# A two-layer graph network on one core: features and first weight ahead of the basis ring, earlier turns, basis parts in pairs

## What is computed

```python
# x [625, 512]; 20625 edges (src, dst, type); D = 512, R = 2 relations, 30 bases
h  = A_norm @ (x @ W0.T) + b            # graph convolution, normalised adjacency
h  = gelu(batch_norm(h)) + x
x  = layernorm(x + h)
def rgcn(x, basis, att, gate_w, root, bias):
    w = einsum('rb,bio->rio', att, basis)       # basis: 30 x 512 x 512 fp32
    msg = sigmoid(x_j @ gate_w[r]) * x_j @ w[r] # x_j: features of each edge's other end
    return segment_sum(msg) + x @ root + bias
out = layernorm(x + rgcn(relu(rgcn(x, ...1)), ...2))
```

## Time and profile before

| | us |
|---|---|
| median of 3 runs | 353.66 (353.53 to 355.02) |
| profiled execution, its own time | 356.38 |
| its span, first to last instruction | 354.5 |
| PE busy | 295.9 (83%) |
| DVE busy | 184.2 (52%) |
| ACT busy | 138.2 (39%) |
| moved by DMA | 73.66 MB, mean 208 GB/s |

### The profile page before, as it was taken

One profiled execution on the slowest core, in us unless ns is written; L12 is line 12 of the kernel. 1 busy time (PEld: TensorE's weight loads), 2 busy tenths in 40 slices (PEclk: granted clock), 3 DMA queues, 4 the chain that ended last, 5 costly groups with the idle time before them and its releaser, 6 DMA issues.

```text
span 354.5 us, 4839 instructions
## 1 busy us (share of the span) xinstructions
PE 295.9 (83%) x1709; PEld 195.7 (55%) x1709; DVE 184.2 (52%) x511; ACT 138.2 (39%) x273; POOL 51.8 (15%) x81
## 2 busy tenths in 40 slices
PE   0662398679999779964899999999999899999980
PEld 0321144346665648742466665556779577777760
DVE  6756079998997864568741013233245325333342
ACT  0064179896997032874823411411131332200000
POOL 5010021311110082027200000000000710010000
PEclk9986579899999759997899999999999999999996
DMA  6799278787577868971999957999200320000111
GB/s 242 292 283 328 96 275 319 251 305 264 203 285 269 325 206 307 336 274 66 329 388 421 379 160 275 358 358 327 92 2 0 87 64 0 2 0 25 32 31 59
DMA packets 12613, 73.66 MB, mean 208 GB/s; under 512 B 1808, under 2 KB 2051, under 8 KB 4396
## 3 DMA queue, kind: packets, MB, share of 16 engines
q1 hardware_dynamic: 9980, 68.49, 53.0%
q0 software_dynamic: 1104, 2.36, 2.5%
q10 hardware_dynamic: 1504, 2.49, 2.2%
HBM read 72.05 MB, written 1.28 MB: 207 GB/s over the span
## 4 chain that ended last, share of the span: by engine, by line
PE 67%; DMA 11%; ACT 7%; DVE 6%; issue 5%; POOL 2%; ACTq 1%; DVEq 0%; POOLq 0%
PE psW L488 15%; DMA xs<-in_x_dram 11%; PE psM L469 10%; PE psM L471 9%; PE psM L470 9%; PE psM L706 6%; PE psM L726 5%; PE psE L560 5%; PE psM L612 3%; ACT oh_diff L776 3%; POOL root_lo L438 1%; DVE AT L1083 1%; PE psM L669 1%; PE psM L639 1%; ACT w L771 1%
## 5 line engine op out<-in xcount | busy, mean ns | idle before, releaser
L488 PE MATMUL psW<-basis_ring,S 128*32 128x512 f32 x512 | 74.1, 671 | 1.6 <-DVEq L980 1.4
L1037 DVE TENSOR_SCALAR oh_key<-iota_f,key 128x320 f16<-128x320 f16 x162 | 45.9, 321 | 20.7 <-PE psE L560 16.9
L1197 DVE SCALAR_TENSOR_TENSOR zg<-psM,gate,zg 125x512 fp32r<-125x512 f32 x20 | 15.0, 750 | 60.3 <-ACT zg L894 60.3
L560 PEld LDWEIGHTS psE<-oh_key,oh_src 128*125 128x125 f16 x162 | 21.7, 148 | 33.9 <-ACT oh_src L782 20.2
L560 PE MATMUL psE<-oh_key,oh_src 128*125 128x320 f16 x162 | 31.5, 333 | 10.5 <-ACT oh_src L782 10.3
L776 ACT ACTIVATE oh_diff<-iota_f,edgeT 128x128 f16<-128x128 f16 x108 | 34.3, 389 | 1.7 <-ACT xT_full L790 0.9
L469 PE MATMUL psM<-w,hlT 128*125 128x512 f32 x80 | 32.7, 409 | 0.1
L894 ACT ACTIVATE zg<-psM,gate 125x512 fp32r<-125x512 f32 x20 | 13.8, 688 | 47.1 <-PE psM L471 46.7
L471 PE MATMUL psM<-w,hlT 128*125 128x512 f32 x80 | 31.6, 395 | 0.0
L470 PE MATMUL psM<-w,hlT 128*125 128x512 f32 x80 | 31.6, 395 | 0.0
L706 PEld LDWEIGHTS psM<-BB,zg 125*128 125x128 f32 x160 | 23.1, 188 | 4.2 <-DVEq L1220 3.4
(11 more groups left out here) (161 smaller groups left out, 445.4 us busy)
## 6 DMA issues: line engine op xcount, KB each, us to landing
basis_ring<-in_L_gnn_basis_dram SPq DMA_DIRECT2D x64, 1024.0 KB, 6.4
root_raw<-in_L_gnn_root_dram POOLq DMA_DIRECT2D x32, 64.0 KB, 2.3
xs<-in_x_dram ACTq DMA_DIRECT2D x1, 1250.0 KB
out_dram<-xs SPq DMA_DIRECT2D x5, 250.0 KB
w_raw<-in_L_gnn_W_dram ACTq DMA_DIRECT2D x1, 1024.0 KB, 39.5
bias_b<-in_L_gnn_bias_dram POOLq DMA_DIRECT2D x1, 250.0 KB, 3.6
rows_i<-in_dst_dram SPq DMA_DIRECT2D x1, 80.0 KB
rows_i<-in_src_dram ACTq DMA_DIRECT2D x1, 80.0 KB
```

The costliest lines, as they stand in the source:

```text
L488: m = nc.tensor.matmul(psW[32 * j:32 * j + 32, cc % 2, :], S[:, cc % 2, cc // CH, q].rearrange("p k r -> p (k r)"), ring[:, n % RING, j, : ...
L560: nc.tensor.matmul(psE[0:PC, g % 2, 0:KEYS], oh_src[:, g % 3, j * P:j * P + PC], oh_key[:, t % OH, :], start=(j == 0), stop=(j == G - 1)). ...
L1037: v.tensor_scalar(oh_key[:, t % OH, :], iota_f[:, 0:KEYS], key[:, t:t + 1], None, ALU.is_equal) \
L1197: link(v.scalar_tensor_tensor(out=zg[:, 1, c, r, :], in0=bank(("Z", L, c, r))[0:PC, :], scalar=gate[:, L, c, r:r + 1], in1=zg[:, 0, c, r, ...
```

## The change

- ACT issues neither `xs` nor `w0_raw`; SP issues them ahead of the ring, `xs` in two pieces of partitions, 112 and 13. The output chunks are stored in the same two pieces.
- B is zeroed by ACT (waited for by DVE through `b_zero`), no longer by POOL.
- `turned` begins with x's chunks 0 and 1. Four turns stand ahead of the edge loop (PE), the other five in groups 0 to 4; ACT evicts two ahead of the loop and one a group in groups 0 to 6. x times W runs in groups 4 to 13. PE's small `base` and `att` matmuls stand behind turns 0 and 1.
- DVE makes the window bases and `key` first; S (8 operations of twice the width instead of 16) and the `more_i` chain follow the twelfth `oh_key`.
- `basis_upto(n)` rounds n up to the odd number, everywhere. In the loop it goes up to 9g/10, with no lead.
- POOL's `vec_rows_q` copy follows its nine subtractions. The tables of the w steps move to later groups, and `w_first(2)` behind the loop.

```diff
+WIDE = PC // 16 * 16
...
-        turned = [("xT", 0)] + [("w0T", k) for k in range(KC)] + [("xT", c) for c in range(1, NC)]
+        turned = [("xT", 0), ("xT", 1)] + [("w0T", k) for k in range(KC)] + [("xT", c) for c in range(2, NC)]
...
-        FIRST_XW = 14
-        TURN_AT = dict(zip((2, 4, 6, 8, 10, 12, 15, 17, 19), range(len(turned))))
-        EVICT_AT = {g + 1: i for g, i in TURN_AT.items()}
-        LEAD = 3
-        FIRST_AT = {2: 0, 13: 1, 23: 2}
-        HIGH_AT = {9: 0, 20: 1}
-        MERGE_AT = {8: 0, 18: 1}
-        LOW_AT = {10: 0, 21: 1}
+        FIRST_XW = 4
+        FIRST_TURNS = 4
+        FIRST_AT = {8: 0, 17: 1}
+        HIGH_AT = {13: 0, 22: 1}
+        MERGE_AT = {11: 0, 20: 1}
+        LOW_AT = {14: 0, 23: 1}
...
             edge_rows(sp, 1, dst)
+            for p in (slice(0, WIDE), slice(WIDE, PC)):
+                sp.dma_start(xs[p], x.rearrange("(c p) o -> p c o", p=PC)[p]).then_inc(x_in, 16)
+            sp.dma_start(w0_raw[:], W0.rearrange("(c p) o -> p c o", p=P)).then_inc(w0_in, 16)
...
-                sp.dma_start(out.rearrange("(c p) o -> p c o", p=PC)[:, c], xs[:, c]).then_inc(out_done, 16)
-            sp.wait_ge(out_done, 16 * NC)
+                for p in (slice(0, WIDE), slice(WIDE, PC)):
+                    sp.dma_start(out.rearrange("(c p) o -> p c o", p=PC)[p, c], xs[p, c]).then_inc(out_done, 16)
+            sp.wait_ge(out_done, 16 * 2 * NC)
...
-            nc.gpsimd.memset(B[:].bitcast(F32), 0.0).then_inc(consts, 1)
...
             def basis_upto(n):
+                n = (n + 1) // 2 * 2 - 1
                 for i in range(parts_done[0], n + 1):
                     basis_part(i)
...
-            basis_upto(LEAD)
+            for i in range(2):
+                turn(i)
...
+            for i in range(2, FIRST_TURNS):
+                turn(i)
             for g in range(NG):
...
-                if g in TURN_AT:
-                    turn(TURN_AT[g])
+                if g + FIRST_TURNS < len(turned):
+                    turn(g + FIRST_TURNS)
...
-                basis_upto(LEAD + 4 * g // 5)
+                basis_upto(9 * g // 10)
...
-            act.dma_start(xs[:], x.rearrange("(c p) o -> p c o", p=PC)).then_inc(x_in, 16)
-            act.dma_start(w0_raw[:], W0.rearrange("(c p) o -> p c o", p=P)).then_inc(w0_in, 16)
...
             act.wait_ge(consts, 4)
-            act.wait_ge(place_ready, 1)
+            counts = B[:].rearrange("p s t n -> p (s t n)").bitcast(F32)
+            nc.scalar.activation(counts, ones_f[0:PC, 0:1].broadcast_to(list(counts.shape)), ACT.Copy, scale=0.0) \
+                .then_inc(b_zero, 1)
...
+            turned_parts(0)
+            turned_parts(1)
+            act.wait_ge(place_ready, 1)
             for g in range(NG):
                 places(g)
...
-                if g >= FIRST_XW + 3 and (g - FIRST_XW - 3) % 2 == 0:
-                    c = (g - FIRST_XW - 3) // 2
+                if g in range(FIRST_XW + 4, FIRST_XW + 4 + 2 * NC, 2):
+                    c = (g - FIRST_XW - 4) // 2
...
-                if g in EVICT_AT:
-                    turned_parts(EVICT_AT[g])
+                if g + 2 < len(turned):
+                    turned_parts(g + 2)
+            w_first(2)
...
+            def build_S():
+                wait_full(dve, "att")
+                att = bank("att")[:, 0:2 * R * SUB].rearrange("p (q l r) -> p l q r", q=SUB, l=2)
+                for i, r in itertools.product(range(2), range(R)):
+                    for l in range(2):
+                        last = v.tensor_tensor(S[:, i, l, :, :, r], mask_k[:].unsqueeze(1).broadcast_to([P, SUB, KB]),
+                                               att[:, l, :, (i + r) % R].unsqueeze(2).broadcast_to([P, SUB, KB]), ALU.mult)
+                link(last)
+                dve.sem_inc(free_dve, 1)
+                link(v.memset(S[0:own(SUB - 1) * KB, :, :, SUB - 1], 0.0))
+                dve.sem_inc(ident_in, 1)
+
+            def rounds():
+                v.tensor_copy(base_i[:], gmm[0:1, 0, :])
+                link(v.tensor_tensor(gmm[0:1, 2, :], gmm[0:1, 1, :], gmm[0:1, 0, :], ALU.subtract))
+                link(v.tensor_reduce(gmm[0:1, 3, 0:1], gmm[0:1, 2, :], AX.X, ALU.max))
+
+                link(v.tensor_scalar(spans[:], iota_f[0:1, 1:MAXW + 1], float(W), gmm[0:1, 3, 0:1], ALU.mult, ALU.is_le))
+                link(v.tensor_reduce(more_f[:], spans[:], AX.X, ALU.add))
+                link(v.tensor_copy(more_i[:], more_f[:]))
...
+                if t == 2 * G - 1:
+                    build_S()
+                    rounds()
+                    dve.wait_ge(b_zero, 1)
                 if t % G == 1 and t > 2 * G:
                     add_window(t // G - 2)
```

## The result

The changed kernel takes **328.68 us** (median of 4 runs, 328.01 to 330.99); the kernel before, run beside it, 354.34 us. The ratio is 0.929, 95% interval 0.923 to 0.934, so 7% faster. The forecast was 326.1 us with a range of 318 to 334. The profiled execution took 328.01 us, its span 326.2 us, for 356.38 and 354.5 us before; for this execution the forecast's sum had been 328.8 us. One execution of one experiment (335.5 us) fell into a slower state, at a granted clock of 0.944, and is left out of that median and range.

The account below looks back on a forecast made before the run. PE's wait for x bounded the start, and PE nearly everything behind the loop. Loop -22.0, pairs -2.8 and end -2.8 us took the profiled 356.38 to 328.8 us; from the median, 353.66 - 27.6 = 326.1 us, range 318 to 334.

Parts of the forecast that it names:

- x's arrival as the bound of the start: Start: PE stands 12.54 us until x lands at 41.59 us, and everything behind x in its stream waits too.
- x lands at 7.5 us: Start: x, issued by SP at 2.00 us, lands at about 7.5 us; bounds 7 and 28 us.
- `base` wait "before DVE asks": Start: `base` queues on PE behind turns 0 and 1, which run 7.5 to about 9.5 us; DVE asks at 10.7 us.
- Parts 0 and 1 in group 0 at 20 to 23 us: Start of the edge loop: PE runs parts 0 and 1, then group 1, at 20 to 23 us, in time for DVE.
- The loop ends at 94 us: Edge loop: its end moves from 116.0 to 94 us, -22.0 us; bounds 89 and 99 us.
- DVE as the bound of the whole loop: Edge loop: DVE becomes the bound throughout, PE close in groups 4 to 13; their coupling costs 1 to 2 us.
- Pairs, -2.8 us: Behind the loop: nine pairs of basis parts replace singles at 0.35 us each; -2.8 us taken, bounds 0 and -4.
- The step to the median: Final sum: the runs' median lies 2.7 us under the profiled execution, so 353.66 - 27.6 = 326.1 us.
- The range: Whole kernel: the forecast holds at 320 to 332 us by the terms' bounds, chance 0.74; stated range 318 to 334 us.
- B (SP held): Rival, start: w0's issue behind x holds SP's queue, PE starts group 2 about 10 us late: 336 us; chance 0.08.
- D: Rival, x and output: the split does nothing, x lands at 22 us, the output gains nothing: 341 us; chance 0.03.
- E, the ring in the pairs: Rival, behind the loop: the basis ring runs dry, 1.2 us waiting on each of 26 pairs: 357 us; chance 0.04.

## Why the prediction was right, and by how much its steps were off

The cause it named is shown. The closeness of the number is luck in two places: it priced a rounding that the change doesn't have, and its errors had opposite signs.

- **x's arrival as the bound of the start:** right. Undoing it alone costs 18 us (346.6 us in one run); doing it alone gives 12.5 us.
- **x lands at 7.5 us:** it was 10.8 us, later also than the 9 us that the profile after was to show. The step took the ring's fastest landing and the rate of 383 GB/s; the chain puts 8.38 us on x's two loads from 2.38 us on. Why they are slower than the ring's was not tried. `rows_f` came at 6.7 us for 5.2, on the last of the edge loads.
- **`base` wait "before DVE asks":** wrong by its consequence. DVE waited 1.18 us for it. With the late x this made `key` 16.7 us instead of 14.5. It cost nothing in the end, as two runs show: with `key` at 13.3 and 16.06 us the last window ended at 97.7 and 97.3.
- **Parts 0 and 1 in group 0 at 20 to 23 us:** wrong, from the misread rounding; they run in group 2, at 28 us. DVE was free for group 2 at 23.7 us for 23 forecast.
- **The loop ends at 94 us:** it ended at 97.1, inside the bounds of 89 and 99; the term is 18.9 us for 22.0. From 23.7 us DVE's work was: groups 55.8, merges 4.9 and low steps 3.8 as reckoned; collisions 4.4 for 4.0, counting the copy. The prediction had added up 92.8 us and allowed 1.2 for coupling. Beyond 92.8 came, roughly, 0.7 us of late start, the 0.4 of collisions, 0.5 us ahead of the first window, about 2 us of waiting for PE in groups 10 and 11, and 0.9 us of waiting for PE's last group (0.86 us in the run without pairs too).
- **DVE as the bound of the whole loop:** half right. It is from group 8 on; up to group 7 ACT, POOL's collisions and DVE share one period of 3.2 us.
- **Pairs, -2.8 us:** the stages behind the loop gave 6.0 us, beyond the bound of -4. The unit price of 0.35 us fits the loss of the run without pairs; what was missing is part 26 (the stretch to agg0 is 2.3 us shorter than in the kernel before), which rounding down takes off the chain, and the shift of parts out of the root1 stage. The sign of that error came from the misreading: of the rounding that the prediction priced, the run that rounds up shows a gain of nothing in these stages, the edge of its bounds. It had also added up 3.4 us (3.1 and 0.3) and taken 2.8 without a reason.
- **The end, -2.8 us:** 3.4 us between the profiles, 2.8 us by the run that undoes it.
- **The step to the median:** the forecast took off 2.7 us, by which the profiled execution before lay above its median. After the change the profiled execution lay 0.7 us under the median. That is why the sum for the profile (328.8) is 0.8 us above the measured 328.0 and the forecast (326.1) 2.6 us under the measured 328.7.
- **The range:** 320 to 332 us is narrower than the bounds behind it. All the unfavourable ones together give 337 us (99 us for the loop, 0 for the pairs, +0.3 at the end).
- **Rivals:** B (SP held) did not come: 0.40 us. Its mechanism is real, though: with x in one piece the same issue on SP takes 5.09 us. D did not come, and the run with x in one piece shows its price, x at 21.9 us where D had 22 us, and 339.1 us for its 341 (which counts the output as well). E, the ring in the pairs, showed itself once in the loop, for 1.0 us, and did not decide, though the prediction had named any wait for `basis_ring` as a sign of being wrong:

```profile
77.76 1.07 PE L490 MATMUL psW<-basis_ring,S 128*32 128x512 f32 x8 [1.00 <-DMA basis_ring<-in_L_gnn_basis_dram]
```

Between the profiles, then, 3.1 us too much in the loop, 3.2 us too little behind it and 0.6 at the end nearly cancelled; the sum was better than its terms.

## What to carry to other kernels

A load that everything waits for should be judged by its place in the queue and by its shape: a first dimension of 125 cost 11 us for 1.28 MB until it was cut into 112 and 13. The busy share of the DMA engines while it is alone in flight (0.33 here) shows such a load. When a long stall goes, add up each engine's whole work in the stretch behind it, with collisions; in this kernel the largest sum was the new bound, and being early on anything else gained nothing. A block of work that is moved in pairs should be priced by where it lands in the stream, not only by what the pair saves.

## What was not expected of the hardware

- The same 1.28 MB from the same queue place: turned at 21.9 us as one transfer of 125 partitions, at 10.8 us as 112 and 13. The issue behind it took 5.09 us in the first case and 0.40 in the second.
- A POOL subtraction of 1.26 us holds whichever DVE instruction meets it, with 128x162 operands (1.27 us for 0.33) as with 128x320 ones, and a POOL operation moved elsewhere takes the collision with it.
- x's early arrival was worth 12.5 us alone and 18 us within the new order. In the new order `key` waits for x through `base`, and x's delay of 17.9 us goes over to it whole.
- After PE had stood for 12.5 us its granted clock was 0.51 for the next 6 us, which cost some 3 us more.
